# Two late residual adds given to GpSimd, bias matmuls moved ahead, and W rounded in another order, in a fused mixing and quantized FFN kernel

## The reference

```python
# x: (64, 64, 512) f32; cond: (64,) rows of a table (200, 64, 64); W: (512, 512); bias: (512,)
w = table[cond]
y = einsum('bct,bcd->bdt', x, w)              # the mixing, per sample
a = quant_dequant_mxfp4(y.reshape(-1, 512))   # blocks of 32 along t: a power of two as scale,
Wq = quant_dequant_mxfp4(W)                   #   elements rounded to e2m1
out = x + (einsum('mk,nk->mn', a, Wq) + bias).reshape(x.shape)
```

## Time and profile before

| what | us |
|---|---|
| median of 3 runs | 96.83 (96.57 to 97.84) |
| the profiled execution's own time | 95.26 |
| its span in the trace | 93.6 |
| DVE busy | 83.2 (89%) |
| PE busy | 81.6 (87%) |
| ACT busy | 74.5 (80%) |
| GpSimd busy | 30.2 (32%) |

### The profile page before, as it was taken

The page is one execution under the profiler, slowest core; times in us unless marked ns, Lnnn a source line. Parts: engine busy times, 40 slices in busy tenths (PEclk is TensorE's granted clock), DMA queues, the critical chain, the costliest instruction groups (busy, mean ns, idle before and its releaser), DMA issues.

```text
span 93.6 us, 2117 instructions
## 1 busy us (share of the span) xinstructions
PE 81.6 (87%) x695; PEld 40.7 (44%) x695; DVE 83.2 (89%) x149; ACT 74.5 (80%) x86; POOL 30.2 (32%) x57
## 2 busy tenths in 40 slices
PE   4998596996899998999899989989989999999600
PEld 4995273592483334332433423343334344335300
DVE  1188989999999999999999999999999999999900
ACT  3736099998997949999999999999999997956000
POOL 4478776997787003002100500040012003030000
PEclk9999999999999999999999999999999999999996
DMA  1988598999999999999999995589179859939894
GB/s 30 334 301 277 124 374 263 352 329 285 333 282 300 347 294 326 194 251 240 270 270 294 329 257 107 224 220 214 42 248 244 159 221 239 210 80 281 318 313 138
DMA packets 14683, 23.20 MB, mean 248 GB/s; under 512 B 4178, under 2 KB 4946, under 8 KB 14674
## 3 DMA queue, kind: packets, MB, share of 16 engines
q1 hardware_dynamic: 11744, 17.83, 63.2%
q0 software_dynamic: 2256, 4.21, 21.3%
q10 hardware_dynamic: 674, 1.05, 3.6%
HBM read 11.54 MB, written 8.39 MB: 213 GB/s over the span
## 4 chain that ended last, share of the span: by engine, by line
PE 46%; ACT 11%; DVE 8%; issue 6%; DVEq 0%; ACTq 0%
PE o_ps L378 24%; PE y_ps L331 6%; ACT o_sb L528 5%; PE o_ps L373 4%; ACT y_sb L507 4%; PE y_ps L378 4%; PE o_ps L359 2%; PE o_ps L343 2%; DVE last_x L809 2%; DVE top L694 2%; DVE a L703 1%; DVE x_sb L804 1%; PE y_ps L359 1%; PE o_ps L405 1%; PE y_ps L343 1%
## 5 line engine op out<-in xcount | busy, mean ns | idle before, releaser
L378 PE MATMUL o_ps<-wT,aT 128*128 128x512 bf16 x104 | 24.9, 380 | 0.0
L331 PE MATMUL y_ps<-x_sb,mix 64*64 64x512 f32 x128 | 16.8, 609 | 4.7 <-ACT y_sb L507 3.2
L675 DVE TENSOR_TENSOR n_int<-y_sb,inv 128x1024 int16<-128x1024 f32 (+1 forms) x18 | 19.6, 1099 | 0.3
L307 POOL DMA_DIRECT2D x_sb<-o_sb x6 | 6.1, 1014 | 41.7 <-ACT o_sb L528 41.7
L499 ACT ACTIVATE z<-y_ps 128x1024 bf16<-128x1024 bf16 x16 | 16.2, 1036 | 3.8 <-PE y_ps L331 3.6
L203 POOL DMA_DIRECT2D mix<-in_L_cond_weights_dram x32 | 16.7, 522 | 5.5 <-issue 4.2
L405 PE MATMUL o_ps<-idle 128*128 128x128 bf16 x202 | 15.3, 243 | 1.2 <-DVE idle L708 1.2
L507 ACT COPY y_sb<-y_ps 128x1024 f32<-128x1024 f32 x16 | 16.3, 1037 | 0.0
L405 PEld LDWEIGHTS o_ps<-idle 128*128 128x128 bf16 x202 | 13.8, 110 | 2.8 <-issue 2.5
L378 PEld LDWEIGHTS o_ps<-wT,aT 128*128 128x128 bf16 x104 | 9.1, 98 | 12.0 <-issue 2.7
L515 ACT ACTIVATE zone<-inv 128x1024 int16<-128x1024 int16 (+1 forms) x13 | 12.0, 941 | 0.3 <-DVE inv L668 0.3
(11 more groups left out here) (59 smaller groups left out, 76.4 us busy)
## 6 DMA issues: line engine op xcount, KB each, us to landing
x_sb<-in_x_dram SPq DMA_DIRECT2D x7, 1024.0 KB, 10.8
out_dram<-x_sb SPq DMA_DIRECT2D x16, 256.0 KB, 3.4
x_sb<-o_sb POOLq DMA_DIRECT2D x6, 512.0 KB, 5.6
out_dram<-x_sb SPq DMA_DIRECT2D x5, 512.0 KB, 2.8
w_sb<-in_L_ffn_weight_dram SPq DMA_DIRECT2D x4, 256.0 KB, 3.7
last_x<-in_x_dram SPq DMA_DIRECT2D x4, 256.0 KB, 8.2
x_sb<-in_x_dram SPq DMA_DIRECT2D x1, 512.0 KB, 6.0
mix<-in_L_cond_weights_dram SPq DMA_DIRECT2D x32, 16.0 KB, 7.5
```

What stands on the lines that cost most here:

```text
L331: last = nc.tensor.matmul(y_ps[HALVES[g], 2 * q + r, :], mix[HALVES[r], (step - 1) * GROUP + n, :], x_tiles(step, n)[HALVES[r], :], start= ...
L378: last = nc.tensor.matmul(o_bank(step, t), aT[:, t, c, :], wT[:, c, :], start=False, stop=(c == KC - 1))
L675: nc.vector.tensor_tensor(columns(n_int, t, n), columns(y_sb[:, step % 2, :, :], t, n), columns(inv, t, n), ALU.mult).then_inc(n_done, 1)
```

## The change

- GpSimd takes over the two residual adds of pair 1 of step 7. ACT's new `copy_later` copies the two tiles from PSUM to the new buffer `late_sb` behind the second turned copy of step 8; GpSimd adds them to x in SBUF in one instruction and issues one store of both tiles (512 KB). DVE's two adds and SP's two stores of 256 KB are gone, and the counts of the waits follow.
- The two bias matmuls of pair 0 leave `ffn_pair` and go ahead of `mix_pair(step + 3, 0)`, with the wait for the bias. Those of pair 1 stay where they were.
- In the hand-written tail, the residual and bias matmuls of pair 0 of step 7 go ahead of both of that step's transposes; before, they stood between them.
- ACT does all four zones of step 8 ahead of `copy_late`; before, the fourth came behind `copy_late` and the first turned copy.
- W's rounding: one tile, `tree_1` of the other pair, one tile, then both last tiles at once; before, both first tiles at once behind `tree_1`, then one and one. `limit` comes ahead of `tree_2(4)`, `rescale` ahead of `tree_3(4)`.

```diff
@@ sync @@
-            for t in range(SUMMED, GROUP):
-                sp.wait_ge(added, t - SUMMED + 1)
-                store(LAST - 1, t)
...
-            sp.wait_ge(late_stored, 16)
+            sp.wait_ge(late_stored, 16 * 2)
@@ gpsimd @@
+            pool.wait_ge(late_copied, 4)
+            late_x = x_tiles(LAST - 1, SUMMED, 2)
+            nc.gpsimd.tensor_tensor(late_x, late_sb[:, :, :].rearrange("p t n -> p (t n)"), late_x, ALU.add
+                                    ).then_inc(late_added, 1)
+            pool.wait_ge(late_added, 1)
+            n0 = (LAST - 2) * GROUP + SUMMED
+            pool.dma_start(out_dram[:, n0:n0 + 2, :], late_x.rearrange("p (n t) -> p n t", n=2)
+                           ).then_inc(late_stored, 16)
@@ tensor @@
+            def bias_pair(step, q):
+                for t in (2 * q, 2 * q + 1):
+                    bias_tile(step, t, start=(q == 1))
             def ffn_pair(step, q):
-                pe.wait_ge(aT_ready, tiles_done(step, 2 * q + 1))
-                for t in (2 * q, 2 * q + 1):
-                    bias_tile(step, t, start=(q == 1))
                 for t in (2 * q, 2 * q + 1):
                     ffn_tile(step, t)
...
                 if step > 1:
-                    for q in range(2):
-                        ffn_pair(step - 1, q)
+                    ffn_pair(step - 1, 0)
+                    pe.wait_ge(aT_ready, tiles_done(step - 1, 3))
+                    bias_pair(step - 1, 1)
+                    ffn_pair(step - 1, 1)
                 mix_pair(step + 2, 1)
...
+                if step == 1:
+                    pe.wait_ge(ones_ready, 1)
+                    pe.wait_ge(bias3_in, 16 * 2 * 3)
+                bias_pair(step, 0)
                 if step + 3 <= LAST:
                     mix_pair(step + 3, 0)
...
+            pe.wait_ge(y_copied, tiles_done(LAST, 1))
+            residual_pair(LAST - 1, 0)
+            bias_pair(LAST - 1, 0)
             pe.wait_ge(y_copied, tiles_done(LAST, 3))
             pe.wait_ge(a2_done, late_part(0))
             turn_pair(LAST - 1, 0, straight=True)
-            residual_pair(LAST - 1, 0)
-            for t in range(2):
-                bias_tile(LAST - 1, t, start=False)
             pe.wait_ge(a2_done, late_part(1))
             turn_pair(LAST - 1, 1)
@@ scalar @@
+            def copy_later():
+                act.wait_ge(o_ready, tiles_done(LAST - 1, GROUP - 1))
+                nc.scalar.copy(late_sb[:, :, :], y_ps[:, SUMMED:GROUP, :]).then_inc(late_copied, 2)
...
-            for t in range(GROUP - 1):
+            for t in range(GROUP):
                 zone_pair(after(LAST), late_part(1), t, 1)
             copy_late()
-            copy_turned_last(0)
-            zone_pair(after(LAST), late_part(1), GROUP - 1, 1)
-            for t in range(1, GROUP):
+            for t in range(GROUP):
                 copy_turned_last(t)
+                if t == 1:
+                    copy_later()
@@ vector @@
+            round_w(0, 1)
             tree_1(0, 2, 2, z_count=GROUP)
-            round_w(0, 2)
+            round_w(1, 1)
...
-            round_w(2, 1)
+            round_w(2, 2)
             tree_1(1)
-            round_w(3, 1)
+            limit(0, 2, 2, 2)
             tree_2(4)
-            limit(0, 2, 2, 2)
+            rescale(0, 2, 3, 2, 2)
             tree_3(4)
-            rescale(0, 2, 3, 2, 2)
...
-            for t in range(SUMMED, GROUP):
-                dve.wait_ge(o_ready, tiles_done(LAST - 1, t))
-                nc.vector.tensor_tensor(x_tiles(LAST - 1, t), o_bank(LAST - 1, t), x_tiles(LAST - 1, t), ALU.add
-                                        ).then_inc(added, 1)
```

More of the change, by code:

```diff
@@ L67, in adaln_ffn_program @@
         last_x = sb("last_x", [P, GROUP, T], F32)
+        late_sb = sb("late_sb", [P, GROUP - SUMMED, N], F32)
         w_sb = sb("w_sb", [P, GROUP * K], F32)
@@ L101, in adaln_ffn_program @@
         x_in = [sem(f"x_in_{s}") for s in range(STEPS + 1)]
-        last_x_in = sem("last_x_in")
+        last_x_in, late_added = sem("last_x_in"), sem("late_added")
         sp_mix_in = [sem(f"sp_mix_in_{s}") for s in range(STEPS + 1)]
@@ L254, in _ @@
                     store(step, SUMMED, GROUP - SUMMED)
-            for t in range(SUMMED, GROUP):
-                sp.wait_ge(added, t - SUMMED + 1)
-                store(LAST - 1, t)
             for t in range(GROUP - 1):
-                sp.wait_ge(added, t + 3)
+                sp.wait_ge(added, t + 1)
                 store_last(sp, t, 0, slice(0, N), stored)
             for half in range(2):
-                sp.wait_ge(added, GROUP + 2 + half)
+                sp.wait_ge(added, GROUP + half)
                 store_last(sp, GROUP - 1, 0, n_half(half), stored)
-            sp.wait_ge(stored, 16 * (2 * (LAST - 1) + LAST - 3 + 2 + GROUP + 1))
+            sp.wait_ge(stored, 16 * (2 * (LAST - 1) + LAST - 3 + GROUP + 1))
             sp.wait_ge(others_stored, 16 * (GROUP + 1))
-            sp.wait_ge(late_stored, 16)
+            sp.wait_ge(late_stored, 16 * 2)
         @block.gpsimd
@@ L392, in ffn_half, with ffn_pair @@
                 last.then_inc(o_ready, 1)
-            def ffn_pair(step, q):
-                pe.wait_ge(aT_ready, tiles_done(step, 2 * q + 1))
+            def bias_pair(step, q):
                 for t in (2 * q, 2 * q + 1):
                     bias_tile(step, t, start=(q == 1))
+            def ffn_pair(step, q):
                 for t in (2 * q, 2 * q + 1):
@@ L422, in _ @@
             for step in range(1, LAST - 1):
-                if step == 2:
-                    pe.wait_ge(ones_ready, 1)
-                    pe.wait_ge(bias3_in, 16 * 2 * 3)
                 if step > 1:
-                    for q in range(2):
-                        ffn_pair(step - 1, q)
+                    ffn_pair(step - 1, 0)
+                    pe.wait_ge(aT_ready, tiles_done(step - 1, 3))
+                    bias_pair(step - 1, 1)
+                    ffn_pair(step - 1, 1)
                 mix_pair(step + 2, 1)
@@ L442, in _ @@
                     residual_pair(step, 0)
+                if step == 1:
+                    pe.wait_ge(ones_ready, 1)
+                    pe.wait_ge(bias3_in, 16 * 2 * 3)
+                bias_pair(step, 0)
                 if step + 3 <= LAST:
                     mix_pair(step + 3, 0)
-            for q in range(2):
-                ffn_pair(LAST - 2, q)
+            ffn_pair(LAST - 2, 0)
+            pe.wait_ge(aT_ready, tiles_done(LAST - 2, 3))
+            bias_pair(LAST - 2, 1)
+            ffn_pair(LAST - 2, 1)
+            pe.wait_ge(y_copied, tiles_done(LAST, 1))
+            residual_pair(LAST - 1, 0)
+            bias_pair(LAST - 1, 0)
             pe.wait_ge(y_copied, tiles_done(LAST, 3))
@@ L451, in _ @@
             turn_pair(LAST - 1, 0, straight=True)
-            residual_pair(LAST - 1, 0)
-            for t in range(2):
-                bias_tile(LAST - 1, t, start=False)
             pe.wait_ge(a2_done, late_part(1))
             turn_pair(LAST - 1, 1)
-            for t in range(2):
-                ffn_tile(LAST - 1, t)
+            ffn_pair(LAST - 1, 0)
             pe.wait_ge(aT_ready, tiles_done(LAST - 1, 3))
[L461 to L464, removed]
+            bias_pair(LAST - 1, 1)
+            ffn_pair(LAST - 1, 1)
             pe.wait_ge(pair_copied, 2 * (LAST - 2))
@@ L596, in _ @@
             copy_turned(LAST - 1, 1)
-            for t in range(GROUP - 1):
+            for t in range(GROUP):
                 zone_pair(after(LAST), late_part(1), t, 1)
             copy_late()
-            copy_turned_last(0)
-            zone_pair(after(LAST), late_part(1), GROUP - 1, 1)
-            for t in range(1, GROUP):
+            for t in range(GROUP):
                 copy_turned_last(t)
+                if t == 1:
+                    copy_later()
             for t in range(GROUP - 1):
-                act.wait_ge(added, t + 3)
+                act.wait_ge(added, t + 1)
                 store_last(act, t, 1, slice(0, N), others_stored)
             for half in range(2):
-                act.wait_ge(added, GROUP + 2 + half)
+                act.wait_ge(added, GROUP + half)
                 store_last(act, GROUP - 1, 1, n_half(half), others_stored)
@@ L727, in _ @@
             tree_3(3, 2, 2)
-            rescale(0, 1, 1, 0, 2)
+            rescale(0, 1, 2, 0, 2)
             block_max(2, 2, 2)
```

## The result

The changed kernel is slower: 97.77 us in the median (96.44 to 99.03, 6 executions) against 96.70 (95.12 to 98.61, 6), a ratio of 1.0172 with a 95% interval of 1.011 to 1.0234. Forecast was 96.6, a change too small to tell. A second series gave 1.0127 (1.006 to 1.0195), so 1.3 to 1.7%, some 1.2 to 1.7 us.

The account below looks back on a forecast made before the run. Three engines within 5% in steady steps, with VectorE's 8.44 us the next limit; at the end GpSimd's landing at 92.85 replaced SP's wait at 93.03, -0.2 us, so 96.83 became 96.6; range 95.2 to 98.1.

Parts of the forecast that it names:

- the sum's last line: End of program: GpSimd's store landing at 92.85 against SP's closing wait at 93.03 before, -0.2 us.
- slipping copies: Rival, chance 0.16: ACT's copies slip, PE's gain doesn't appear, copy_later ends 0.5 to 1 us later; +0.5, 97.3.
- Rival B: GpSimd's late add much dearer than DVE's; at 4.4 us, landing at 95.2, +2.1 us, 98.9; chance 0.12.
- VectorE as the bound of the steady steps, bias worth 0.13 us: Steps 2 to 5: PE gains 1.1 to 1.2 us, DVE keeps 8.44 a step and regains only 0.13.
- W's rounding, 0.1 us (bounds 0 and 0.3): DVE in step 1: one rounding fewer behind tree_1, partly lost to waits; gain 0.1 us.
- Residual and bias ahead of the transposes, ffn_pair(7, 0) 0.4 to 0.5 earlier, and 0.5 lost by the order: Tail on PE: of its 1.0 us lead 0.4 to 0.5 survives; ffn_pair(7, 0) can start at 78.0.
- VectorE's last add at 87.8 and 88.2 its end: Tail on DVE: end at 88.2 instead of 88.89, 0.45 us from PE and some 0.25 from DVE's queue.
- the fourth zone: ACT's tail: zone ahead of copy_late, hidden by ACT's idle 0.98 us; DVE's last limit has it long before.
- Both queues' stores landed by 91.7: SP's and ACT's last stores: without two late stores SP issues until about 89.3, all landing by about 91.7.
- GpSimd's start at 85.05: Tail: GpSimd's late add starts 0.3 us behind copy_later's end at 84.75.
- GpSimd's add, 2.1 (bounds 1.28 and 2.6): Late add of 128 x 1024 f32 on GpSimd takes 2.1 us, between DVE's adds and scaled affine_select.
- Landing 5.6 us behind the issue: GpSimd's late 512 KB store: issued at 87.25, 5.6 us to landing at 92.85, from earlier 5.1 and 5.9.

Follow-up runs that it names:

- e3: Kernel before with GpSimd's part alone (late adds and store by GpSimd, copy_later by ACT); 1.0188 (1.0139 to 1.0238) against the kernel before.
- e5: Kernel before plus a 2 KB SBUF copy issued by GpSimd behind VectorE's last add; 1.0122 (1.0058 to 1.0186) against the kernel before.
- e13: Changed kernel with GpSimd's late store cut from 512 KB to 2 KB, output incomplete; 0.9886 (0.9837 to 0.9935) against the kernel before.
- e1: Changed kernel with the late 512 KB store issued by SP, GpSimd still adding; 1.0045 (0.9987 to 1.0104) against the kernel before.
- e11: Kernel before with only the loop's bias matmuls of pair 0 moved ahead of the mixing; one execution, 96.48 us.
- e9: e6 with residual and bias of pair 0 of step 7 back between the transposes; 0.9973 (0.993 to 1.0017) against the kernel before.
- e10: e6 with SP also storing pair 1 of step 6 in place of GpSimd; 1.0044 (1.0006 to 1.0083) against the kernel before.
- e8: Changed kernel with GpSimd's add but without the late store, two tiles never output; 0.9878 (0.983 to 0.9925) against the kernel before.
- e14: Changed kernel run again, nothing altered; 1.0127 (1.006 to 1.0195) against the kernel before.
- e2: Changed kernel without GpSimd's part, VectorE's two adds and SP's two stores back; 0.9979 (0.993 to 1.0027) against the kernel before.
- e7: As e6, VectorE adding, but GpSimd issues the one late 512 KB store; 1.0025 (0.9981 to 1.0069) against the kernel before.
- e6: e2 with one late 512 KB store by SP instead of two of 256 KB; 0.997 (0.9933 to 1.0006) against the kernel before.
- e4: Kernel before plus a 2 KB SBUF copy by GpSimd behind VectorE's first add to last_x; 0.9976 (0.9927 to 1.0025) against it.

## Why the prediction was wrong, step by step

**The step that failed** is the sum's last line, 92.85 - 93.03 = -0.2 us. It set the landing of GpSimd's DMA against the end of SP's wait and let the rest of the span follow in 0.57 us for either. For SP's and ACT's stores that held (93.03 to 93.6). For a DMA of GpSimd the end of the program comes about 2.2 us behind the landing: 95.06 to 97.3 in the changed kernel, 92.95 to 95.1 in e3. Put 2.2 in place of 0.57 and the forecast landing gives 95.05 instead of 93.4, +1.45 us, or 1.5%, inside both intervals. The row for it was in the trace of the kernel before, a drain of 7811 ns at 82.8 that nobody waited for; I didn't look at the instructions behind the program's last wait. That the measured median, 97.77, lies between 95.2 and 98.1 is no credit: the upper part of that range was there for a dear add and for slipping copies, and neither came; the ratio taken of 96.83 gives 98.5. Rival B found the right sign and the wrong cause: the add took 2.35 us, not 4.4.

**How much of the loss is the drain** is shown only in part. e5 shows that a late drain costs without late bytes (1.2% by its times, 0.8 us by its trace). In the changed kernel's trace it ends 0.9 us behind SP's. SP's own end, at 96.1 (aligned 94.3 against 93.4 before), gives the other 0.9. It goes with the late 512 KB: in e13, where these are 2 KB, SP had drained at 94.3 from nearly the same tree_1 of step 3 (30.11). By the trace the drain is half of the loss. e1, with the bytes and without the late drain, is 0.45% slower than before, the changed kernel 1.3 to 1.7%, and by that it is two thirds to three quarters; but e1's interval holds a loss of nothing too. Nearer than that it isn't known.

**VectorE as the bound of the steady steps, bias worth 0.13 us**: right (0.12 in the changed kernel's trace, 0.11 in e11's).

**W's rounding, 0.1 us (bounds 0 and 0.3)**: from tree_1 of step 1 to that of step 2 it is 8.47 us before and 24.00 - 15.73 = 8.27 after; 8.01 to 8.36 in the eleven traces with the edit, 8.40 to 8.47 in the five without. Some 0.2, inside the bounds.

**Residual and bias ahead of the transposes, ffn_pair(7, 0) 0.4 to 0.5 earlier, and 0.5 lost by the order**: wrong. Aligned it starts at 78.26, 0.13 earlier, and e9 shows that the order costs nothing. The old order waits 0.74 us for VectorE's rescale of the first pair, the new one 0.51 us for that of the second, and ffn_pair follows 49.9 us behind tree_1 of step 3 in both. I had part of TensorE's 1.0 us of lead survive the tail, where a rescale of VectorE is the limit in either order.

**VectorE's last add at 87.8 and 88.2 its end**: wrong in both terms, and near in size by luck. Aligned the add ends at 88.55, and with 0.2 us from W's rounding at 88.35. TensorE's ffn_pair(7, 0) came 0.13 us earlier and not 0.45, and the 0.25 from VectorE's queue aren't there (59.79 us with GpSimd's adds, 59.82 with VectorE's). Besides the 0.12 of the steady steps, about 0.2 us came from a term that I had priced at nothing, the fourth zone. Before, VectorE's last limit started at 84.26, as that zone ended at 83.60 + 0.63, 0.53 us behind the rescale ahead of it; with the zone moved it follows 0.34 us behind:

```profile
83.73 0.42 DVE L703 TENSOR_TENSOR a<-n_int,top 128x512 bf16<-128x512 int16 x1
...
84.26 0.42 DVE L694 TENSOR_TENSOR top<-zone,s 128x512 bf16<-128x512 bf16 x1
```

```profile
85.46 0.41 DVE L718 TENSOR_TENSOR a<-n_int,top 128x512 bf16<-128x512 int16 x1
...
85.80 0.41 DVE L709 TENSOR_TENSOR top<-zone,s 128x512 bf16<-128x512 bf16 x1
```

The distance is 0.53 in e3 and e11 too, which lack the edit, and 0.34 in e9 and e10, which have it.

**Both queues' stores landed by 91.7**: wrong by over 2 us. SP's wait ended at 95.83, aligned 94.0. I took SP's issuing as the bound, since its instructions stood back to back, and its seven issues became five; but the five took from 87.39 to 93.02, 5.63 us instead of 3.64. Some 1.5 us of that are waits for VectorE's adds, which TensorE now spreads out, and the last issue alone took 2.07 us. It took 0.6 in e8 and e13, which lack the late 512 KB, and in the kernel before; all five took 4.1 to 4.2 us in e8 and e13, and 4.9 in e14, which has the bytes. So the length of an issue was no fixed price: it was longer with more bytes on their way. e8, with 512 KB less, ends 3.7 us behind the last add instead of 4.6 to 5.4. That is why 0.7 us on VectorE gave 0.2% in e2.

**GpSimd's start at 85.05**: 85.07 aligned, by two errors that cancel. copy_later ended at 84.98 instead of 84.75, and GpSimd started 0.09 us behind it instead of 0.3. **GpSimd's add, 2.1 (bounds 1.28 and 2.6)**: 2.35; the estimate by proportion from the Trainium skill's page "GPSIMD Engine Reference" (section Elementwise — side-by-side cycle accounting), 2.25, was nearer. The wait on late_added took 0.30 us instead of 0.1. **Landing 5.6 us behind the issue**: 5.5 and 5.4 in the changed kernel, 4.5 in e3 and 4.8 in e7, where the page "DMA: Bandwidth & Descriptors" of the Trainium skill leads to an estimate of 3.2. For the late store that is not borne out, nor for 2 KB, which took 2.8 to 3.4. GpSimd's store of step 6, of the same 512 KB, did come near it in e7, e8 and e9, with 3.3 to 3.4, and took 4.6 to 6.3 in the other traces.

**What stays open.** What the drain of GpSimd waits for: 1.9 to 2.0 us behind the landing of its last DMA fit all fourteen traces of the table and e1, and e8 doesn't. Why the accumulating DMA of step 6 takes 2 us longer in some traces. And no version that computes the whole result beat the kernel before clearly: e6 and e9, at 0.3% faster, reach 1 with their intervals.

## What to carry to other kernels

Ask of any work given to GpSimd near the end not only when its data land, but when GpSimd is done with the program: here the end came 2.2 us behind the landing of its last DMA, against 0.6 behind the end of SP's wait for its stores. Read the instructions behind the last wait of the kernel before: a closing drain that is hidden by 3 us will not stay hidden when its DMA moves 5 us later. And where the last microseconds are stores, an engine that finishes 0.7 us earlier buys little; e8 and e13 show what does, fewer bytes left to store by then. And before work is taken off an engine, look at what it will wait for instead: VectorE lost 1.28 us of adds and waited 0.98 us for TensorE.

## What the hardware showed that was not expected

- GpSimd's closing drain lasts 4.8 to 9.6 us in these traces, SP's 7 ns. The Trainium skill's page "VectorE: DVE Perf Modes" (section The DRAIN you can't avoid) gives the drains of a program's preamble and postamble as some 12 ns on all five engines. SP's is of that order; the other engines' closing drains were longer (ScalarE 0.4 to 0.6 us, VectorE 0.5 to 0.7, TensorE 1.4 to 1.5), and the measurement decides, for GpSimd above all.
- A DMA of 2 KB from GpSimd, whose landing held nobody up (in e5 at 93.09, where SP's wait for its stores ended at 94.1), made the kernel 1.2% slower (e5) or left it as it was (e4), depending only on whether it was issued at 89.7 or 87.6.
- TensorE's mean granted clock at 10 to 15 us was 0.66 in five traces (changed, e8, e11, e13, e14), 0.73 in e7 and 1.00 in the other ten. In the changed kernel's trace TensorE had idled 1.9 us just before, and the 16 matmuls took 3.63 us where they had taken 1.95. The idle time alone doesn't set it: e1 had idled 2.2 us and e5 2.0, and both kept 1.00 and 1.95 us.
